# A selective scan on one core: du is replicated one pair further ahead than dt, and ScalarE scales the inputs of the next pair before it turns to that pair's exponential

## What is computed

```python
def step(h, inp):
    u_t, dt_t, B_t, C_t = inp
    dA = jnp.exp(jnp.clip(dt_t[..., None] * A, -20.0, 0.0))
    dB_u = jnp.clip(dt_t[..., None] * B_t[:, None, :] * u_t[..., None], -10.0, 10.0)
    h = jnp.clip(h * dA + dB_u, -100.0, 100.0)
    y = jnp.einsum('bds,bs->bd', h, C_t)
    return (h, y)
```

## Time and profile before

| | |
|---|---|
| median of 3 runs | 7111.94 us (7104.16 to 7112.86) |
| profiled execution, its own time | 7101.98 us |
| its span | 7100.3 us |
| mean granted clock of PE | 0.822 of full speed |
| scan: first L1973 to last L1983 | 4874.1 to 6438.6 us from the span's start |
| DVE L1973, L1983 | 2048 instructions each, 766.3 us and 787.5 us busy |
| ACT L1937, L1943 | 557.1 us and 644.3 us busy |
| POOL L1858 | 512 instructions, 584.3 us busy |

### The profile page before, as it was taken

The page is one execution under the profiler, slowest core; times in us unless marked ns, Lnnn a source line. Parts: engine busy times, 40 slices in busy tenths (PEclk is TensorE's granted clock), DMA queues, the critical chain, the costliest instruction groups (busy, mean ns, idle before and its releaser), DMA issues. The chain is left out here.

```text
span 7100.3 us, 100514 instructions
## 1 busy us (share of the span) xinstructions
PE 5536.8 (78%) x27676; PEld 2718.0 (38%) x27676; DVE 5608.7 (79%) x10599; ACT 4495.3 (63%) x7377; POOL 1522.4 (21%) x2039
## 2 busy tenths in 40 slices
PE   7979979799897989979689974443666666666778
PEld 4445445444454445544356642220111111113555
DVE  6777687776777777777688868887999999996768
ACT  6666666666666657666444446666777777775443
POOL 0000000000000000000011114444444343334421
PEclk8999999899998999989899986665555555557989
DMA  0000000000000000000011113332111111113432
GB/s 21 0 12 0 1 12 0 13 0 1 12 0 13 0 12 0 0 7 0 21 39 41 40 56 117 117 115 85 42 44 43 44 42 44 43 44 119 154 106 71
DMA packets 198774, 271.75 MB, mean 38 GB/s; under 512 B 13989, under 2 KB 157989, under 8 KB 192454
## 3 DMA queue, kind: packets, MB, share of 16 engines
q1 hardware_dynamic: 181190, 252.90, 11.7%
q10 hardware_dynamic: 17408, 16.78, 0.7%
HBM read 151.14 MB, written 118.49 MB: 38 GB/s over the span
## 5 line engine op out<-in xcount | busy, mean ns | idle before, releaser
L613 DVE TENSOR_REDUCE at_nmax<-at_ps_s 128x1 f32<-128x1024 f32 x1024 | 1246.1, 1218 | 299.1 <-PE at_ps_s L331 288.2
L374 PEld LDWEIGHTS at_ps_t<-identf,at_qk 128*128 128x128 f32 x8192 | 886.2, 141 | 749.5 <-issue 615.1
L460 ACT ACTIVATE at_qk<-at_ps_s,at_nmax 128x1024 f32<-128x1024 f32 x1024 | 1155.5, 1128 | 5.9 <-DVE at_nmax L613 5.9
L374 PE MATMUL at_ps_t<-identf,at_qk 128*128 128x128 f32 x8192 | 1126.3, 281 | 8.6 <-DVE at_probsT L623 8.6
L471 ACT COPY at_probsT<-at_ps_t 128x512 f32<-128x512 f32 x1024 | 603.0, 589 | 798.4 <-PE at_ps_t L374 797.9
L346 PE MATMUL at_ps_o<-at_probsT,at_vh 128*32 128x512 f32 x4096 | 1072.5, 612 | 0.0
L1884 PE MATMUL sc_da<-sc_parts,sc_sel 24*128 24x512 bf16 x1024 | 527.2, 616 | 596.5 <-DVE sc_decayed L1973 506.9
L623 DVE COPY at_probsT<-at_ps_t 128x512 f32<-128x512 f32 x1024 | 705.5, 689 | 350.4 <-PE at_ps_t L374 336.2
L1983 DVE CUSTOM_DVE_ANT_0 sc_state<-sc_xd,sc_decayed 128x256 f32<-128x256 f32 x2048 | 787.5, 426 | 136.1 <-POOL sc_xd L1858 135.7
L1937 ACT ACTIVATE sc_da<-sc_da,sc_a_col 128x1024 f32<-128x1024 f32 x512 | 557.1, 1088 | 375.1 <-PE sc_da L1884 375.0
L1858 POOL TENSOR_SCALAR sc_xd<-sc_xd 128x1024 f32<-128x1024 f32 x512 | 584.3, 1141 | 942.3 <-ACT sc_xd L1943 942.3
(11 more groups left out here) (300 smaller groups left out, 8432.4 us busy)
## 6 DMA issues: line engine op xcount, KB each, us to landing
dt_parts<-si_pt SPq DMA_DIRECT2D x64, 384.0 KB, 2.6
du_parts<-si_pu SPq DMA_DIRECT2D x64, 384.0 KB, 3.2
sc_parts<-dt_parts SPq DMA_DIRECT2D x128, 192.0 KB
sc_parts<-du_parts SPq DMA_DIRECT2D x128, 192.0 KB
u_tok<-si_ut SPq DMA_DIRECT2D x8, 2048.0 KB, 8.3
y<-sc_yo SPq DMA_DIRECT2D x256, 64.0 KB
so_yin<-y SPq DMA_DIRECT2D x32, 512.0 KB
so_uin<-u_tok SPq DMA_DIRECT2D x32, 512.0 KB
```

The source lines that it names most:

```text
L374: last = nc.tensor.transpose(ps_t[hf][:, c * P:(c + 1) * P], probs[:, t % 2, (hf * 4 + c) * P:(hf * 4 + c + 1) * P], identf[:])
L460: nc.scalar.activation(probs[:, t % 2, :], ps_s[t % 2][:], ACT.Exp, bias=nmax[:, t % 2:t % 2 + 1], accum_out=rsum[:, hd, t:t + 1]).then_in ...
L613: nc.vector.tensor_reduce(nmax[:, t % 2:t % 2 + 1], ps_s[t % 2][:], AX_X, ALU.max, negate=True).then_inc(s_max, 1)
```

## The change

On PE, `replicate` is split. `replicate_dt` does the two matmuls of dt(n) in a row; `replicate_du` does the two of du. In turn q PE now does dt of pair q+2 and then du of pair q+3. On ACT the pair's step is split too: `decays(n)` is the exponential of pair n, `inputs(n + 1)` the two copies for the next pair, and `inputs(0)` goes ahead of the loop. The number of instructions, their shapes and their buffers stay, and nothing is changed on DVE, POOL or SP.

```diff
-            def replicate(it, q, first=False):
+            def replicate_dt(it, q, first=False):
...
                 if not first:
                     pe.wait_ge(s_dec, (n - 1) * 2 * NC)
                 for j in range(2):
-                    bank = slice(j * HALF, (j + 1) * HALF)
-                    dt_done = nc.tensor.matmul(da[q % 2][:, j], sel[0:KR, :], parts[0:KR, h, q % HP * 2 + j],
-                                               start=True, stop=True)
-                    if j == 1:
-                        dt_done.then_inc(s_rdt, 1)
+                    last = nc.tensor.matmul(da[q % 2][:, j], sel[0:KR, :], parts[0:KR, h, q % HP * 2 + j],
+                                            start=True, stop=True)
+                last.then_inc(s_rdt, 1)
+
+            def replicate_du(it, q, first=False):
...
+                for j in range(2):
                     if not (first and q == 0):
                         pe.wait_ge(s_xd, 2 * n - 1 + j)
-                    du_done = nc.tensor.matmul(ps_du[:, bank], sel[Q1:Q1 + KR, :],
-                                               parts[Q1:Q1 + KR, h, q % HP * 2 + j], start=True, stop=True)
-                du_done.then_inc(s_rdu, 1)
+                    last = nc.tensor.matmul(ps_du[:, j * HALF:(j + 1) * HALF], sel[Q1:Q1 + KR, :],
+                                            parts[Q1:Q1 + KR, h, q % HP * 2 + j], start=True, stop=True)
+                last.then_inc(s_rdu, 1)
...
+                    if q + LEAD + 1 < NPAIR:
+                        replicate_du(it, q + LEAD + 1)
+                    elif not last:
+                        replicate_du(it + 1, q + LEAD + 1 - NPAIR)
...
+            def decays(n, q):
+                act.wait_ge(s_rdt, n + 1)
+                flat = da[q % 2][:].rearrange("p j d -> p (j d)")
+                nc.scalar.activation(flat, flat, ACT.Exp, scale=a_col[:]).then_inc(s_da, 1)
+
+            def inputs(n, q, fresh=False):
+                act.wait_ge(s_rdu, n + 1)
+                if not fresh:
+                    act.wait_ge(s_state, (n - RING + 1) * 2 * NC)
+                for j in range(2):
+                    nc.scalar.activation(xd[:, q % RING, j], ps_du[:, j * HALF:(j + 1) * HALF], ACT.Copy,
+                                         scale=bt[:, bass.ds(2 * n + j, 1)]).then_inc(s_xd, 1)
+
             def turn(it, g, first, last):
                 for q in range(NPAIR):
                     n = it * NPAIR + q
...
+                    decays(n, q)
+                    if not (last and q == NPAIR - 1):
+                        inputs(n + 1, q + 1, first and q + 1 < RING)
                     if q == HP - 1 and not first:
                         store(it - 1, 1 - g)
 
+            inputs(0, 0, True)
             schedule(act, turn)
```

More of the change, by code:

```diff
@@ L1877, in replicate @@
                 if q % HP == 0:
-                    for c in range(2):
-                        pe.wait_ge(s_in[h][c], 16 * it + 16)
+                    pe.wait_ge(s_in[h][0], 16 * it + 16)
                 if not first:
@@ L1882, in replicate @@
                 for j in range(2):
-                    bank = slice(j * HALF, (j + 1) * HALF)
-                    dt_done = nc.tensor.matmul(da[q % 2][:, j], sel[0:KR, :], parts[0:KR, h, q % HP * 2 + j],
-                                               start=True, stop=True)
-                    if j == 1:
-                        dt_done.then_inc(s_rdt, 1)
+                    last = nc.tensor.matmul(da[q % 2][:, j], sel[0:KR, :], parts[0:KR, h, q % HP * 2 + j],
+                                            start=True, stop=True)
+                last.then_inc(s_rdt, 1)
+            def replicate_du(it, q, first=False):
+                n = it * NPAIR + q
+                h = q // HP
+                if q % HP == 0:
+                    pe.wait_ge(s_in[h][1], 16 * it + 16)
+                for j in range(2):
                     if not (first and q == 0):
                         pe.wait_ge(s_xd, 2 * n - 1 + j)
-                    du_done = nc.tensor.matmul(ps_du[:, bank], sel[Q1:Q1 + KR, :],
-                                               parts[Q1:Q1 + KR, h, q % HP * 2 + j], start=True, stop=True)
-                du_done.then_inc(s_rdu, 1)
+                    last = nc.tensor.matmul(ps_du[:, j * HALF:(j + 1) * HALF], sel[Q1:Q1 + KR, :],
+                                            parts[Q1:Q1 + KR, h, q % HP * 2 + j], start=True, stop=True)
+                last.then_inc(s_rdu, 1)
             def add_y(it, g, r):
@@ L1908, in turn @@
                     if q + LEAD < NPAIR:
-                        replicate(it, q + LEAD)
+                        replicate_dt(it, q + LEAD)
                     elif not last:
-                        replicate(it + 1, q + LEAD - NPAIR)
+                        replicate_dt(it + 1, q + LEAD - NPAIR)
+                    if q + LEAD + 1 < NPAIR:
+                        replicate_du(it, q + LEAD + 1)
+                    elif not last:
+                        replicate_du(it + 1, q + LEAD + 1 - NPAIR)
                     if q % 2 == 1:
@@ L1915, in _ @@
             for q in range(LEAD):
-                replicate(0, q, first=True)
+                replicate_dt(0, q, first=True)
+            for q in range(LEAD + 1):
+                replicate_du(0, q, first=True)
             schedule(pe, turn)
```

## The result

The changed kernel takes 7340.83 us (median of 4 runs, 7336.38 to 7345.17), the kernel before, on the same chip, 7112.27: a ratio of 1.0324 with a 95% interval of 1.0306 to 1.0342. It is slower by 228.6 us. Its profiled execution took 7336.38 us with a span of 7334.7, against 7100.3, a difference of 234.4.

What follows compares the result with a forecast made beforehand. DVE was taken as nearly the bound, with its waits for POOL's clip and their mutual lock. 512 x (3.52 - 3.054) = +239 us on 7101.98 gave 7341, plus 9.96 to the median: 7351; range 7100 to 7385.

Steps and rivals of the forecast that it cites:

- What bounds it: In the scan, DVE nearly the bound, busy 182.45 of 200 us; its waits for the clip, 134.1 us, would end.
- The chain from D to the clip: D is the recorded end of a pair's last L1973 on DVE; POOL's clip asks 3.48 us later, as before.
- The lock and its three cases: POOL's clip, asking p after an L1983 group's start, stalls DVE by s: 0.84, 0.17, or 0.17 to 0.90 us.
- Rival 3: DVE is held until POOL's recorded end: stall 0.96, 3.64 us per pair, 7412 us; chance 0.04.
- rival 2: No contention between POOL's clip and DVE for early inputs: 2.68 us per pair, 6921 us; chance 0.04.
- The slow solution: The clip asks 0.04 after an L1983 group's start, stalling DVE 0.84; time per pair P = 3.52 us; chance 0.70.
- How it starts: At the scan's start clip(2) blocks pair 1's first L1983 by some 0.7; its second then starts within 0.05 of clip(3).
- PE's new order hides behind DVE: On PE, y starts 1.5 after a pair's last L1973 ends; PE is free at 3.4 to 3.48, dt due at 3.57.
- Rival 1: Faster: the clip asks about 0.66 after an L1983 group; 2.90 us per pair, 2.995 with dt late, 7082; chance 0.14.
- P = 2.68, 6921: Time per pair and total, in us, with DVE alone as the limit and no stall from POOL's clip.
- light cycle: The clip asks about 0.66 after an L1983 group, stall 0.22, 2.90 us per pair; undamped, lost by a stall over 0.55.
- 191 us to be had: At first sight 0.37 us x 512 pairs, from taking inputs and clip off the way to DVE's state.

Runs made afterwards that it cites:

- four places tried: The changed kernel as it is, 7340.83 us, and with POOL's clip held to three points of DVE's progress: 7031.09, 7169.38 and 7334.09 us.
- both later held places: The changed kernel with POOL's clip held until DVE finished L1983's second half, 7169.38 us, or the following L1973's first half, 7334.09 us.

## Why the prediction was right, and where it wasn't

- **What bounds it, and that the semaphore wait would go.** Right: no wait of DVE for the clip is left.
- **The chain from D to the clip, 3.48.** Right to 0.01, and dt 0.06 after D where 0.05 was given.
- **The lock and its three cases.** Right at all four places tried, to 0.01. Of the rule of the Trainium skill (SBUF — State Buffer, section "Who interferes with whom") the runs bear out the exclusion. To the letter, with DVE blocked until the POOL instruction has finished, s would be 0.98; it is 0.84. Rival 3 falls with that, and rival 2 with the 1.59.
- **The slow solution, p = 0.04 and P = 3.52.** p is 0.04 and P 3.507. That makes 7 of the 10 us by which the forecast was high (512 x 0.013); the rest lies at the two ends of the scan, where the sum counted full cycles too.
- **How it starts.** Right: the block of some 0.7 on pair 1's first state group, and the next one beginning within 0.05 of clip(3) (0.01). That this start decides, and nothing else in the order, is shown by the run with three held clips and by the delayed clip in the kernel before.
- **PE's new order hides behind DVE.** Right at P = 3.51. y starts 1.56 after D (5391.22, given 1.5), but that agreement is luck: y waited there for the stretched state group, which ends at 5389.59 + 1.58 = 5391.17, and not for du, whose last matmul had begun at 5390.31, 0.65 after D and not 0.9 to 1.0. du's matmuls ran beside dt's in the new order too: dt at 5389.72 and 5390.12, du at 5389.92 and 5390.31. That the order costs nothing in itself is shown by the two kernels without a clip.
- **Rival 1.** Its mechanism is real, its time was put too high: 7044 measured for 7082. I had given dt's lateness behind y 0.095 per pair on top of 2.90; the measured mean is 2.927 in all.
- **"P = 2.68, 6921" if the clip cost nothing.** Wrong, and the one place where the reasoning missed a bound: with no clip at all P is 2.897 and the time 7026 to 7028. I had taken DVE for the next limit, and for the light cycle seen dt's place behind y, but had not closed the ring through the inputs and du's one buffer. So of the "191 us to be had" only some 86 were there, wherever the clip falls, as long as PE and ACT keep this ring; with y ahead of du it is 104.

Open: where exactly the edge of the light cycle lies, between stalls of 0.45 and 0.61, and how far the ring could be shortened.

## What to carry over

An engine that no longer waits has not become free: look at the length of its instructions as well as at its idle time, and compare each with the same instruction undisturbed. When a periodic loop has an instruction on another engine that shares a resource with it, work out where it falls in the period and whether that place reproduces itself; there can be more than one such cycle, and a change that only shifts the start can choose the bad one for the whole loop. Tie such an instruction to the progress of the engine it disturbs (one wait, 310 us here), or cut it to the size of the gap.

## What the hardware showed that was not expected

- A delay of 0.50 us once, in pair 20 of 512, changed the time of all the pairs after it from 3.03 to 3.51 us.
- A POOL instruction that asks while DVE's first half runs gets in ahead of the second half, although DVE issues its halves back to back: a 0.75 us group takes 1.59.
- DVE is let in before POOL's recorded end: a clip of 1.04 us holds it for 0.90, in the change and in both later held places alike. DVE's decays, with one input in PSUM, are not held: 1021 of them run inside a clip in the kernel before, and none takes over 0.426.
- From the recorded end of the DVE instruction that signals to the start of a waiting POOL instruction there were some 0.16 us (p 0.57, 0.90 and 1.24).
